# A post-norm attention and MoE layer in one kernel: the attention front with biases and residual by matmul, K, V and sums read from PSUM, K*V before its rotation, and Q between the K/V tiles

## The reference

```python
# attention part
QKV = einsum('bsd,ed->bse', X, W_in) + b_in ; Q, K, V = split(QKV, 3)
Q = rope(Q, 128) ; K = rope(K, 128)          # rotary embedding of the first 128 features
A = sum(feature_map(K) * V, axis=-2)         # feature_map: each row of K over its norm; A has 256 numbers
Y = einsum('bsd,ed->bse', A[:, None, :] * Q, W_out) + b_out
x = layernorm(x + (Y + x))
# feed-forward part: 8 experts, 2 of them weighted per token, all computed
probs = softmax(x @ gate_w) ; two largest, normalised, times alpha -> combine
h = gelu(x @ fc1_w[e] + fc1_b[e]) ; y = h @ fc2_w[e] + fc2_b[e]
x = layernorm(x + sum_e combine[:, e] * y[e])
```

## Time and profile before

| | us |
|---|---|
| runs, median (lowest to highest of 3) | 152.05 (151.35 to 152.91) |
| span of the profiled execution | 150.5 |
| PE busy in it | 135.8 |
| DVE busy in it | 105.7 |
| ACT busy in it | 77.3 |
| POOL busy in it | 67.6 |

### The profile page before, as it was taken

The page is one execution under the profiler, slowest core; times in us unless marked ns, Lnnn a source line. Parts: engine busy times, 40 slices in busy tenths (PEclk is TensorE's granted clock), DMA queues, the critical chain, the costliest instruction groups (busy, mean ns, idle before and its releaser), DMA issues.

```text
span 150.5 us, 2427 instructions
## 1 busy us (share of the span) xinstructions
PE 135.8 (90%) x802; PEld 118.9 (79%) x802; DVE 105.7 (70%) x233; ACT 77.3 (51%) x146; POOL 67.6 (45%) x81
## 2 busy tenths in 40 slices
PE   4999979955999899999999999999999999999920
PEld 4778859825987579897898998998998998989910
DVE  0549899996598938899955965745965654638991
ACT  4515966017076894168064264264265265297571
POOL 3004899913999807048306606707507606000310
PEclk9999997555599999999999999999999999999996
DMA  4899940000003130004000400400300000000034
GB/s 133 213 321 419 387 185 4 0 0 0 2 4 121 44 119 0 0 0 139 4 0 0 139 4 2 139 0 0 139 0 0 0 0 0 4 0 0 0 121 158
DMA packets 4698, 10.55 MB, mean 70 GB/s; under 512 B 545, under 2 KB 2641, under 8 KB 4433
## 3 DMA queue, kind: packets, MB, share of 16 engines
q1 hardware_dynamic: 4688, 10.43, 20.1%
HBM read 9.38 MB, written 1.05 MB: 69 GB/s over the span
## 4 chain that ended last, share of the span: by engine, by line
PE 64%; DVE 20%; DMA 5%; ACT 3%; SPq 3%; issue 1%; ACTq 0%; DVEq 0%
PE ps L878 21%; PE ps L879 20%; PE ps L880 20%; DMA wq<-in_w_q_t 5%; DVE z L607 4%; DVE qa L648 2%; DVE kv L588 2%; SPq L257 2%; DVE x L727 2%; DVE z L678 1%; ACT gT_lo L425 1%; DVE stats L849 1%; DVE fT_lo L699 1%; DVE qb L656 1%; DVE acc L752 1%
## 5 line engine op out<-in xcount | busy, mean ns | idle before, releaser
L738 DVE TENSOR_TENSOR gT_lo<-kv,gT_hi 128x512 fp32r<-128x512 f32 x30 | 26.1, 884 | 26.1 <-ACT gT_hi L509 26.0
L352 POOL TENSOR_TENSOR w_hi<-wraw,zero 128x512 fp32r<-128x512 f32 x16 | 18.9, 1181 | 41.2 <-PE ps L880 41.2
L878 PE MATMUL ps<-w_hi,gT_hi 128*128 128x256 f32 x120 | 33.7, 281 | 0.1
L880 PE MATMUL ps<-w_hi,gT_lo 128*128 128x256 f32 x120 | 33.4, 279 | 0.0
L879 PE MATMUL ps<-w_lo,gT_hi 128*128 128x256 f32 x120 | 33.4, 278 | 0.0
L878 PE MATMUL ps<-fT_hi,w_hi 128*128 128x512 f32 x64 | 25.5, 399 | 0.3 <-DVE fT_lo L699 0.3
L879 PE MATMUL ps<-fT_lo,w_hi 128*128 128x512 f32 x64 | 25.4, 396 | 0.0
L880 PE MATMUL ps<-fT_hi,w_lo 128*128 128x512 f32 x64 | 25.3, 395 | 0.0
L507 ACT ACTIVATE kv<-ps,b_now 128x512 f32<-128x512 f32 x16 | 11.0, 690 | 24.7 <-PE ps L880 24.5
L878 PEld LDWEIGHTS ps<-w_hi,gT_hi 128*128 128x128 f32 x120 | 22.7, 189 | 1.1 <-issue 0.4
L752 DVE SCALAR_TENSOR_TENSOR acc<-ps,comb,acc 128x256 f32<-128x256 f32 x53 | 22.6, 475 | 1.0 <-PE ps L880 0.7
(11 more groups left out here) (139 smaller groups left out, 243.1 us busy)
## 6 DMA issues: line engine op xcount, KB each, us to landing
wraw<-in_expert_w SPq DMA_DIRECT2D x8, 512.0 KB, 3.4
xT<-in_x_t SPq DMA_DIRECT2D x4, 256.0 KB, 5.6
acc<-in_x_tok SPq DMA_DIRECT2D x1, 1024.0 KB, 9.5
rT<-in_rope_t SPq DMA_DIRECT2D x1, 1024.0 KB, 10.8
out<-z SPq DMA_DIRECT2D x4, 256.0 KB, 2.2
wkv<-in_w_kv_t SPq DMA_DIRECT2D x2, 256.0 KB, 3.6
rtok<-in_rope_tok SPq DMA_DIRECT2D x1, 512.0 KB, 7.8
brow<-in_b_rows SPq DMA_DIRECT2D x1, 384.0 KB, 6.4
```

Of the source, the lines that this page charges most:

```text
L352: g.tensor_tensor(w_hi[:, slot, cols], src, zero[:].to_broadcast([P, 2 * D]), ALU.add).then_inc(w_part, 1)
L738: v.tensor_tensor(low, h[:, i, :], raw(high), ALU.subtract).then_inc(g_lo_ok, 1)
L878: nc.tensor.matmul(dst, lh, rh, start=k == 0, stop=False)
L880: last = nc.tensor.matmul(dst, ll, rh, start=False, stop=k == len(terms) - 1)
```

## The change

- Loads: `x_tok` is gone. The bias comes as 33 rows (row 0 and row 32 filled, zeros between), 101 KB instead of 384 KB. Cosines (`cs`) and sines (`sn`) are two loads; the sines land in `sn[:, :, 1, :]`, in pieces of 64 numbers. ACT issues the first two `x_t` loads.
- Bias: POOL splits the rows into `b_parts` (high in row 0, low in row 32), DVE makes `pick` (ones in rows 0 and 32), and a seventh matmul `pick * b_parts` in each K/V tile adds it. PE waits for `b_lo_ok` ahead of the first of these.
- K and V stay in PSUM. ACT squares K there and copies only V (`vs`). DVE multiplies K by V, and the halves of K crosswise by V (`m2`). POOL (tiles 0 to 6) and DVE (tile 7) turn these by cosine and sine behind the product. `feature_sum` has three matmuls for each tile instead of two, and all eight tiles stand in one row behind `q_block(1, 0)`.
- `q_block(0, 0)` and `q_block(0, 1)` stand between K/V tiles 3 and 4. DVE rotates Q from PSUM, bias included.
- Residual: `residual(t)` is five matmuls of 256 columns (x times 2*I, and the output bias); `attend(t)` is the former product. Sums stay in PSUM (`z_ps`), and statistics and `normalise` read them there.
- The second and third pair: `normalise(1)` stands ahead of `x1_high(0)`, and `normalise(2)` ahead of `x1_high(1)`; `x1_low` handles a pair at a time. The five idle matmuls ahead of expert 0 are gone.
- The sqrt table of ACT is loaded at the start.

```diff
@@ SP
-            sp.dma_start(wkv[:, 0, :], w_kv_t[:, 0, :]).then_inc(l_wkv[0], 16)
-            load_x_t(0)
-            sp.dma_start(wkv[:, 1, :], w_kv_t[:, 1, :]).then_inc(l_wkv[1], 16)
-            load_x_t(1)
-            sp.dma_start(brow[:], b_rows.partition_broadcast(P)).then_inc(l_brow, 16)
+            for k in range(KD):
+                sp.dma_start(wkv[:, k, :], w_kv_t[:, k, :]).then_inc(l_wkv[k], 16)
             load_x_t(2)
+            sp.dma_start(braw[:], b_rows).then_inc(l_bias, 16)
             load_x_t(3)
-            sp.dma_start(rtok[:], rope_tok).then_inc(l_rtok, 16)
+            sp.dma_start(cs[:], rope_tok[:, 0, :, :]).then_inc(l_cs, 16)
+            sp.dma_start(sn[:, :, 1, :], rope_tok[:, 1, :, :]).then_inc(l_sn, 16)
             sp.dma_start(wq[:], w_q_t).then_inc(l_wq, 16)
-            sp.dma_start(acc[:], x_tok).then_inc(l_x, 16)
@@ POOL
+            pool.wait_ge(l_bias, 16)
+            pool.wait_ge(b_zero, 1)
+            g.tensor_copy(b_parts[0:BIAS_K, :], braw[:]).then_inc(b_hi_ok, 1)
+            pool.wait_ge(b_hi_ok, 1)
+            g.tensor_tensor(b_parts[low, :], braw[low, :], raw(b_parts[low, :]), ALU.subtract).then_inc(b_lo_ok, 1)
@@ DVE
+            def kv_product(t):
+                bank = KV_BANK[t]
+                dve.wait_ge(ksq_ok, t + 1)
+                dve.wait_ge(v_ok, t + 1)
+                v.tensor_tensor(z[:, t, :], ps[:, bank, 0:D], vs[:, t, :], ALU.mult).then_inc(m_ok, 1)
+                v.tensor_tensor(m2[:, t, EVEN], ps[:, bank, ODD], vs[:, t, EVEN], ALU.mult).then_inc(turn_ok, 1)
+                v.tensor_tensor(m2[:, t, ODD], ps[:, bank, EVEN], vs[:, t, ODD], ALU.mult).then_inc(turn_ok, 1)
@@ PE
+                if t == 0:
+                    pe.wait_ge(pick_ok, 2)
+                    pe.wait_ge(b_lo_ok, 1)
+                nc.tensor.matmul(ps[:, bank, :], pick[:], b_parts[:, 0:2 * D], start=False, stop=True).then_inc(kv_mm, 1)
...
+                nc.tensor.matmul(rest, z[:, t, ROT:D], norm, start=t == 0, stop=t == T - 1)
+                nc.tensor.matmul(rot, acc[:, t, 0:ROT], norm, start=t == 0, stop=False)
+                return nc.tensor.matmul(rot, acc[:, t, ROT:D], norm, start=False, stop=t == T - 1)
...
+            for t in range(TPH):
+                kv_tile(t)
             pe.wait_ge(wq_lo_ok, 1)
             q_block(0, 0)
             q_block(0, 1)
-            pe.wait_ge(kv_ok, T)
-            feature_sum(0)
+            for t in range(TPH, T):
+                kv_tile(t)
             q_block(1, 0)
-            feature_sum(1).then_inc(a_mm, 1)
+            for t in range(T):
+                last = feature_sum(t)
+            last.then_inc(a_mm, 1)
             q_block(1, 1)
+            def residual(t):
+                z_t = z_ps(t)
+                for k in range(KD):
+                    nc.tensor.matmul(z_t, fT_hi[:, k, tile(t)], twice[:, k, :], start=k == 0, stop=False)
+                    nc.tensor.matmul(z_t, fT_lo[:, k, tile(t)], twice[:, k, :], start=False, stop=False)
+                nc.tensor.matmul(z_t, pick[:], b_parts[:, 2 * D:3 * D], start=False, stop=False)
...
+            residual(0)
+            residual(2)
             pe.wait_ge(wo_lo_ok, KD)
+            attend(0)
+            residual(1)
+            attend(1)
...
-            stay_warm(WARM_NORM)
             pe.wait_ge(w1_ok, 1)
             pe.wait_ge(x1_lo_ok, TPH)
```

More of the change, by code:

```diff
@@ L410, in x_high @@
                 a.copy(fT_hi[:, :, part], xT[:, :, part]).then_inc(xT_hi_ok, 1)
+            for c in range(2):
+                part = slice(c * 256, (c + 1) * 256)
+                act.dma_start(xT[:, :, part], x_t[:, :, part]).then_inc(l_xT[c], 16)
+            act.wait_ge(const_ok, 1)
+            a.activation(table_unused[:, 0:1], eps[:], ACT.Sqrt)
             for k in range(KD):
@@ new lines, in _ @@
+            for t in range(TPH):
+                k_norm(t)
+                v_out(t)
+            k_root(0)
+            act.wait_ge(l_cols, 16)
+            q_pass_high(0)
+            k_norm(4)
+            v_out(4)
+            q_rot_high(0)
+            for t in range(5, T):
+                k_norm(t)
+                v_out(t)
+            k_root(1)
+            act.wait_ge(q_mm, 3)
+            a.activation(qT[ODD, 1, half(1)], ps[ODD, Q_BANK[1][0], :], ACT.Identity,
+                         bias=bq[ODD, 0:1]).then_inc(q_raw_ok, 1)
@@ L898, in _ @@
                     f_hi, f_lo = fT_hi[:, k, tile(t)], fT_lo[:, k, tile(t)]
-                    nc.tensor.matmul(ps[:, t % 4, :], f_hi, wkv_hi[:, k, :], start=k == 0, stop=False)
-                    nc.tensor.matmul(ps[:, t % 4, :], f_hi, wkv_lo[:, k, :], start=False, stop=False)
-                    last = nc.tensor.matmul(ps[:, t % 4, :], f_lo, wkv_hi[:, k, :], start=False, stop=k == KD - 1)
-                last.then_inc(kv_mm, 1)
-            def q_block(n, m):
-                bank = Q_BANK[n][m]
-                if bank < 4:
-                    pe.wait_ge(kv_ok, 4 + bank + 1)
-                product(ps[:, bank, :], [(wq_hi[:, k, tile(m)], wq_lo[:, k, tile(m)],
-                                          fT_hi[:, k, half(n)], fT_lo[:, k, half(n)]) for k in range(KD)])\
-                    .then_inc(q_mm, 1)
@@ L913, in feature_sum @@
-            def feature_sum(n):
-                pe.wait_ge(krec_ok, n + 1)
-                for t in range(n * TPH, (n + 1) * TPH):
-                    pe.wait_ge(kv_prod, t + 1)
-                    for k in range(KD):
-                        last = nc.tensor.matmul(ps[:, 2 + k, 0:1], z[:, t, tile(k)], krec[:, t:t + 1],
-                                                start=t == 0, stop=t == T - 1)
-                return last
+                    nc.tensor.matmul(ps[:, bank, :], f_hi, wkv_hi[:, k, :], start=k == 0, stop=False)
@@ new lines, in kv_tile @@
+                    nc.tensor.matmul(ps[:, bank, :], f_hi, wkv_lo[:, k, :], start=False, stop=False)
+                    nc.tensor.matmul(ps[:, bank, :], f_lo, wkv_hi[:, k, :], start=False, stop=False)
+                if t == 0:
+                    pe.wait_ge(pick_ok, 2)
+                    pe.wait_ge(b_lo_ok, 1)
+                nc.tensor.matmul(ps[:, bank, :], pick[:], b_parts[:, 0:2 * D], start=False, stop=True).then_inc(kv_mm, 1)
+            def q_block(n, m):
+                product(ps[:, Q_BANK[n][m], :], [(wq_hi[:, k, tile(m)], wq_lo[:, k, tile(m)],
+                                                  fT_hi[:, k, half(n)], fT_lo[:, k, half(n)]) for k in range(KD)])\
+                    .then_inc(q_mm, 1)
```

446 lines of the change are left out of this document (228 added, 218 removed).

## The result

The changed kernel takes 161.71 us (median of 4 runs, 160.89 to 162.59), the kernel before 151.70 (151.27 to 152.91) beside it: the ratio is 1.065, with a 95% interval of 1.059 to 1.071. The profiled execution took 161.64 us with a span of 159.6 us, 9.1 more than before. In these two traces 8.8 of the 9.1 us are there when PE starts `fc1(0, 0, 1)`: 62.50 us against 53.70.

A forecast was written before the change was run, and what follows sets the result against it. TensorE, busy nearly everywhere but waiting for VectorE before 35.6 us, bounds it. First statistics at 40.4 plus 16.7 gives 57.1 against 53.7: 3.4 more, span 153.9, plus 1.55 makes 155.5 us; range 151.0 to 159.5.

The forecast's parts named there:

- rival B: The stand for the bias in tile 0 also costs the clock: 2.3 us added, 157.8 us; chance 0.22.
- the sum: Table: the token sum's 24 one-column matmuls, 6.7 us. As failed step: adding the pieces up to 155.5 us.
- from A to the first statistics: From A, the finished sum over tokens at 33.3 us, to the first layernorm statistics at 40.4: 7.1 us.
- rival D: The stand ahead of expert 0, without fillers, costs the clock: 1.7 to 2.7 us added, 157.5 us; chance 0.10.
- piece 1: K/V and Q: PE stands 2.5 us for the bias; `q_block(1, 0)` ends at 26.6 us against 25.4.
- piece 4: Layernorm chain: from first statistics to `fc1(0, 0, 1)` 16.7 us, where it was 14.8.
- How the numbers follow: Splits chance between forecast (0.33) and four rivals; total odds faster 0.16, within 1% 0.19, slower 0.65.
- B with D: Clock lost behind both the tile 0 stand and the stand ahead of expert 0; placed above the range's 159.5 us.
- Rival A: Clock holds through the token sum: 151.7 us, or 149.9 with the bias early too; chance 0.27 (0.13 and 0.14).
- step 2: Sum over tokens: 24 matmuls in one row, 5.4 us; clock falls some 4 us in, making 6.7 us.
- step 4: Layernorm: the ACT and DVE order makes one chain; first fc1 10.6 us behind first statistics, where it was 8.2.
- Rival C: Sines loaded in 256-byte pieces delay `wq`; PE waits about 1.7 us for `wq_lo`: 157.2 us; chance 0.08.

The follow-up runs named there:

- e8: Changed kernel with one 128x512 filler matmul behind the three one-column matmuls of each of tiles 0 to 6 in the sum: 164.42 us.
- e5: Changed kernel with 12 filler matmuls in K/V tile 0, ahead of the wait for the bias parts: 159.70 us, ratio 1.048.
- e4: Changed kernel with 12 filler matmuls behind `attend(7)`, ahead of expert 0's first fc1 block: 159.66 us, ratio 1.048.
- e2: Changed kernel with the sum over tokens split into four pieces between other matmuls: 159.86 us, ratio 1.049.
- e3: Changed kernel with ACT's earlier layernorm order, `x1_high(0)` ahead of `normalise(1)` and `x1_high(1)` ahead of `normalise(2)`: 158.00 us, ratio 1.039.
- e6: Changed kernel with bias matmuls of tiles 0 to 2 later, the sum in four pieces and ACT's earlier layernorm order: 151.46 us, ratio 0.996.
- e11: e6 plus tile 3's bias matmul late, two products added before the sum, and separate banks for sum and Q: 149.84 us, ratio 0.983.

## Why the prediction was wrong

The direction and the places were right; the size was not. In its own steps:

| step of the prediction | forecast | measured | |
|---|---|---|---|
| bias parts ready | 11.2 | 11.5 | copy 1.3 us instead of 0.8 (in e8, with the same front, 0.8), rows there at 7.96 instead of 8.3 |
| end of `q_block(1, 0)` | 26.6 | 28.6 | +2.0: the bias 0.4, rival B 1.4, and 0.2 more at full clock |
| the sum | 6.7 | 7.4 | +0.7; the first slower matmul 3.0 us in, not 4 |
| from A to the first statistics | 7.1 | 7.5 | +0.4 |
| from there to the first fc1 | 10.6 | 11.0 | +0.4; two shifts on DVE took 0.66 and 0.90 us instead of 0.16 |
| from fc1 to `fc1(0, 0, 1)` | 6.1 | 8.1 | +2.0: rival D 1.6, and 0.4 more at full clock |
| rest of the span | 96.8 | 97.1 | +0.3 |
| median above span | 1.55 | 2.1 | +0.5 |

**The step that failed** is the sum: piece 1 counts the stand for the bias, and piece 4 the stand ahead of fc1, by their length alone, and both put the clock behind them at nothing. It was left to rivals B (0.22) and D (0.10), of which "How the numbers follow" lets one come true. But they are independent terms of one sum: B asks what a stand at 8 us does, D what one at 52 us does. Both came true, and e5 and e4 show them at 1.4 and 1.6 us, with nothing else changed. These 3.0 us are half of the 6.2 by which the median missed; with them alone it would have been 158.5, inside the range. The other half is small errors that all had one sign (the bias 0.4, the sum 0.7, the rest in the table), for which a range that took in "B with D" (159.5) only as its very edge had no room.

For B I weighed a stand of 2.5 us against "2.7 us at 21 us", which was no stand of that length: it was 0.87 us of waiting and then one-column matmuls, so it says nothing either way. The stand became 3.1. For D I gave 0.10, although I had worked out a stand of 2.6 us myself. The earlier trace rows show half clock for some 6 us behind a stand of 3.51, though there the clock had been down before it.

Three readings of the prediction were loose and changed nothing. Of slices 6 to 12 only 6, 9 and 10 have PE clearly idle. The spacing of 512-column matmuls in the earlier trace rows is 0.24 us, not 0.23; the changed kernel's trace has 0.227, as the working used it. And the row of the sum is nine times the 25 ns for each matmul, but only 4.5 times the 1.2 us that the prediction worked out for two passes.

**What held.** Of the prediction's signs most came: the stand in tile 0, half clock behind the sum, 11.0 us to the first fc1. The first statistics, at 43.46, came behind its 39 to 42 us. Rival A did not come: the clock fell in the sum, as step 2 had it from the earlier trace rows, and e2 shows what that cost: 4.1 us in all, against the 3.8 between the forecast and A. How far into the row it fell was partly luck, since it varied from 2.4 to 4.8 us. A one-column matmul cost 0.22 us at full clock, as from the earlier trace rows, and not the 25 ns of the Trainium skill's table for its columns (TensorE: Matmul & The Clock Gate, Back-to-back issue gap), a figure for single matmuls that by the same section leaves the weight loads out. The 24 took 7.4 us. The single chain of step 4 was right to 0.4 us, and e3 gives 2.3 us back by order alone. Rival C did not come: `wq_hi` was started at 11.46 us, and the sines landed 6.5 us after their issue, the cosines 6.0. The freed DVE was worth nothing by itself in this order, as forecast: PE was busy without a break from 15 to 50 us.

**What the change had to give.** The rebuilt front isn't worse by nature. With its stands shortened it is 2.1 us ahead of the old one at `fc1(0, 0, 1)` (e6), and with 16 matmuls in the sum and banks of its own 1.7% faster in the end (e11). About 10 us of three repaired losses lay between.

## What to carry to other kernels

Write down every stand of the bottleneck engine that a change makes, and price each twice, for its length and for the clock behind it; add them up, rather than giving each a chance as if one excluded the others. An early wait that all work queues behind was mended here by order alone: the engine does the products of the next tiles first. When a wait is taken away, look for the next one in what the work needs (here a PSUM bank still being read), which the profile may show without a releaser.

## What was unexpected of the hardware

- The clock fell while PE was busy throughout. In the changed kernel it went from 0.96 to 0.50 inside a row of one-column matmuls without a gap, and a 128x512 matmul behind every three of them didn't prevent it (e8). The Trainium skill (TensorE: Matmul & The Clock Gate, HAM oscillation — how this bites in real kernels) tells of a clock that is lost while PE waits some 3 to 5 us for data. The stands here, 3.1 and 2.9 us, are at the low end of that or just below, and the clock was lost behind both; the sum, without any wait, is a case that it doesn't tell.
- On POOL an operation on one partition cost as much for each column as one on 128: 1x768 took 2.11 us (2.7 ns a column), 128x512 in `w_lo` 1.27 to 1.30 (2.5 ns).
- DVE's shift of 128x2 took 0.16 us in one place and 0.66 and 0.90 us in two others. In both of these it ended within 0.02 us of an operation of POOL that was splitting weights (at 45.66 and 48.03 us), and in e3 one of 1.26 us ended at 51.27, POOL's at 51.26. The statistics, which read PSUM, kept their 0.75 us beside the same work. Why is not shown.
